# The second attention of a batch runs inside the mixture half of the other batch

## The chip, the cores and the metric

The kernel runs on one core of one Trainium2 chip. The metric is the device time of one execution in microseconds (us), lower is better. The engines are PE (TensorE), DVE (VectorE), ACT (ScalarE), POOL (GpSimd) and SP (SyncE, which here only issues DMAs). Each engine works through its own instructions in order, and waits on semaphores that others raise.

## The reference

Two batches of 1024 tokens, width 256, pass four sublayers, each `x = layernorm(x + f(x))`: a causal attention (16 heads of 128), a mixture of experts, a second attention, and a second mixture.

```python
x = _layernorm(x + _L0_attn_ref(x, ...))
x = _layernorm(x + _L0_ffn_ref(x, ...))      # 8 experts, top 2, plus a shared expert of 704
x = _layernorm(x + _L1_attn_ref(x, ...))
x = _layernorm(x + _L1_ffn_ref(x, ...))      # 16 experts, top 6, plus a shared expert of 352
# second attention: 16 heads of 16, 4 groups of keys and values, no mask
scores = jnp.einsum('bqhd,bkhd->bhqk', q, k) / HD
out = jnp.einsum('bhqk,bkhd->bqhd', jax.nn.softmax(scores, axis=-1), v).reshape(b, s, D)
return out @ Wout + bout
# a mixture: every expert is computed for every token and weighted
h = jax.nn.silu(xf @ W1.T + B1) * (xf @ W3.T + B3)
y = y + c[:, None] * (h @ W2.T + B2)
```

The second attention mixes tokens of one batch only, and a mixture mixes no tokens at all. So work of batch 0 and of batch 1 in different sublayers is independent.

## The kernel before

Every product of near-fp32 precision is made of three fp32r matmuls (`mm3`): each operand is split into a rounded part (`xh`, `hi_gu`, `hh`, rounded by ACT) and the rest (`xl`, `lo_gu`, `hl`, subtracted by DVE or POOL).

The program is a row of stages, each a block that all engines enter and leave together:

- `causal_attention` (a0), both batches.
- `mixture` f0, first batch 0, then batch 1. A tile K is 128 hidden columns of the experts or of the shared expert: 17 tiles for each batch. For each K the weights are loaded, rounded by ACT (`round_gu`, `round_dn`) and subtracted by POOL once, and used for two chunks c of 512 tokens. A chunk of a tile is 18 matmuls of 512 columns: 6 for `gate`, 6 for `up`, 6 for `down`. `gate_ps` and `up_ps` are banks of their own. ACT applies Silu (L1327), DVE multiplies (`product`, L1385) and weighs by the router's map (L1390), ACT rounds (`keep_hi`, L1338), DVE subtracts (`keep_lo`, L1396). Small "side" tasks (norms n0b and n1a, router r0b, projections x0) are done between the chunks, by a plan written out by hand.
- `in_turn` p1: the norm n1b and projections x1 of batch 1, with no other work beside them; SP then copies keys (`x_ks`) and queries (`a_qq`) into their places.
- `grouped_attention` a1: 16 units (batch, 4 heads, 512 queries) of 16 steps. It begins with 24 leading steps of maxima alone (`FIRST`). A step makes the row maxima of a later unit (`maxima`: two matmuls of 512 keys into one of two pairs of banks, one DVE reduction over 1024, L1675), and the transposed scores of this unit (`scores`: two matmuls, L1568, into one of three banks; ACT takes the exponential, L1656). Every second step adds `values` (L1579, four instructions, eight records). In step 9 of a unit (`TURN`) the unit before is normed and the next maxima are transposed.
- `in_turn` p2: output projection o1a, norm n2a and router r1a of batch 0.
- `mixture` f1, batch 0, then batch 1, 25 tiles for each, with the side tasks o1b, n2b, r1b and n3a.
- `in_turn` p3: the last norm and the stores.

What sets the order is each engine's own list; a matmul that waits holds all later ones up.

## Time and profile before

| | us |
|---|---|
| median of 3 runs | 2251.52 (2243.45 to 2257.3) |
| profiled execution, its own time | 2240.75 |
| its span, first to last instruction | 2238.6 |
| PE busy | 2125.4 (95% of the span) |
| DVE busy | 1455.6 (65%) |
| ACT busy | 1207.5 (54%) |
| POOL busy | 556.9 (25%) |

The span is what the trace covers; 2.15 us of the execution lie around it. Busy times of PE overlap from one matmul to the next, so that 95% does not mean that the array is full.

### The profile page before, as it was taken

The numbers are of one execution on the slowest core, as the hardware profiler recorded it, in microseconds if no ns is written. First come the engines' busy times: TensorE is split into PE (matmuls) and PEld (weight loads), VectorE is DVE, ScalarE is ACT, GpSimd is POOL, SyncE is SP. The second block draws the span as 40 slices with busy tenths as digits, with TensorE's granted clock in tenths as the row PEclk, the third lists the DMA queues.
The fourth block names the chain that finished last, engine by engine and source line by source line (L and its number), as shares of the span: only waits on it lengthen the run. The fifth ranks groups of instructions, "written<-read, shape, count | busy, mean of one in ns | idle before, by whom it ended". The sixth has DMA issues, their size and how long they took to land. (4 is left out here: it accounts for less than half of the span.)

```text
span 2238.6 us, 30499 instructions
## 1 busy us (share of the span) xinstructions
PE 2125.4 (95%) x11008; PEld 1608.0 (72%) x11008; DVE 1455.6 (65%) x2505; ACT 1207.5 (54%) x2425; POOL 556.9 (25%) x543
## 2 busy tenths in 40 slices
PE   7999999999999999989999968999998699999998
PEld 5888888888888888867788853333333487787886
DVE  4666666666766666656656547888883656645554
ACT  5655556565656565534444442877777334434344
POOL 3433434343424343322222210000000012221221
PEclk9999999999999999999999995999999799999999
DMA  2000000000000000011111120100000011111111
GB/s 80 15 9 24 15 24 15 24 15 24 8 24 15 24 15 15 6 31 46 43 43 43 43 42 16 23 16 22 16 22 1 27 36 43 43 50 43 48 45 61
DMA packets 54297, 64.74 MB, mean 29 GB/s; under 512 B 9179, under 2 KB 34566, under 8 KB 54150
## 3 DMA queue, kind: packets, MB, share of 16 engines
q1 hardware_dynamic: 54150, 62.81, 10.1%
q8 instruction: 89, 1.46, 0.3%
q14 instruction: 58, 0.48, 0.1%
HBM read 52.68 MB, written 2.10 MB: 24 GB/s over the span
## 5 line engine op out<-in xcount | busy, mean ns | idle before, releaser
L830 POOL TENSOR_TENSOR a_pr<-a_pr,a_rinv 128x128 f32<-128x128 f32 (+7 forms) x256 | 294.2, 1149 | 514.9 <-DVE a_rinv L1063 514.7
L1675 DVE TENSOR_REDUCE a_negm<-psum 128x1 f32<-128x1024 f32 x256 | 301.4, 1219 | 49.2 <-PE psum L1553 48.4
L1227 POOL TENSOR_TENSOR f_lo_gu<-f_raw_gu,f_hi_gu 128x512 fp32r<-128x512 f32 x84 | 108.9, 1296 | 848.4 <-ACT f_hi_gu L1313 848.4
L1656 ACT ACTIVATE a_pt<-psum 128x512 f32<-128x512 f32 x512 | 268.2, 602 | 81.8 <-PE psum L1568 81.5
L86 PE MATMUL psum<-xh,f_hi_gu 128*128 128x512 f32 x672 | 269.4, 401 | 7.0 <-DVE f_hid L1385 6.8
L1396 DVE TENSOR_TENSOR f_hl<-f_hid,f_hh 128x512 fp32r<-128x512 f32 x168 | 116.6, 694 | 236.6 <-ACT f_hh L1338 234.8
L88 PE MATMUL psum<-xh,f_lo_gu 128*128 128x512 f32 x672 | 263.8, 393 | 0.0
L87 PE MATMUL psum<-xl,f_hi_gu 128*128 128x512 f32 x672 | 263.5, 392 | 0.0
L1327 ACT ACTIVATE f_act_s<-psum,f_bias 128x512 f32<-128x512 f32 x168 | 115.1, 685 | 270.6 <-PE psum L88 270.4
L979 ACT ACTIVATE a_pth<-psum 128x512 fp32r<-128x512 f32 (+3 forms) x384 | 174.7, 490 | 142.9 <-PE psum L886 140.5
L972 ACT ACTIVATE a_pr<-psum,a_negm 128x128 f32<-128x128 f32 (+7 forms) x256 | 190.4, 744 | 81.8 <-DVE a_negm L1054 76.9
L1553 PE MATMUL psum<-x_ks,a_qq 48*128 48x512 f32 x512 | 186.3, 475 | 19.3 <-DMA a_qq<-x_qlo 14.5
L1070 DVE TENSOR_TENSOR a_ptl<-psum,a_pth 128x512 fp32r<-128x512 f32 (+3 forms) x384 | 200.3, 549 | 6.1 <-ACT a_pth L979 5.7
L1054 DVE TENSOR_REDUCE a_negm<-psum 128x1 f32<-128x128 f32 (+7 forms) x256 | 189.5, 741 | 2.9 <-PE psum L876 0.7
L1338 ACT ACTIVATE f_hh<-f_hid 128x512 fp32r<-128x512 f32 x168 | 105.5, 628 | 158.9 <-DVE f_hid L1390 151.8
L886 PE MATMUL psum<-ident,a_pr 128*128 128x128 f32 x1152 | 171.8, 276 | 10.7 <-POOL a_pr L830 9.0
L1568 PE MATMUL psum<-a_qq,x_ks 49*128 49x512 f32 x512 | 171.2, 480 | 4.5 <-ACT a_pt L1656 4.1
L1568 PEld LDWEIGHTS psum<-a_qq,x_ks 49*128 49x128 f32 x512 | 67.8, 187 | 138.5 <-ACT a_pt L1656 136.6
L86 PEld LDWEIGHTS psum<-xh,f_hi_gu 128*128 128x128 f32 x672 | 127.3, 189 | 40.2 <-DVE f_hid L1385 10.2
L1385 DVE SCALAR_TENSOR_TENSOR f_hid<-psum,f_bias,f_act_s 128x512 f32<-128x512 f32 x168 | 125.2, 745 | 43.8 <-PE psum L88 33.5
L1091 DVE TENSOR_TENSOR a_zl<-psum,a_zh 128x512 fp32r<-128x512 f32 x64 | 44.2, 691 | 161.5 <-ACT a_zh L1003 161.5
L1553 PEld LDWEIGHTS psum<-x_ks,a_qq 48*128 48x128 f32 x512 | 95.8, 200 | 74.4 <-DVE a_negm L1675 44.5
(299 smaller groups left out, 4823.4 us busy)
## 6 DMA issues: line engine op xcount, KB each, us to landing
f_raw_gu<-in_gu SPq DMA_DIRECT2D x84, 256.0 KB, 2.7
...
a_qq<-x_qhi SPq DMA_DIRECT2D x128, 32.0 KB, 2.0
...
```

Of the source, the lines that this page charges most:

```text
L86: pe.matmul(out, a_hi, b_hi, start=first, stop=False)
L87: pe.matmul(out, a_hi, b_lo, start=False, stop=False)
L88: return pe.matmul(out, a_lo, b_hi, start=False, stop=last)
L830: pool.tensor_tensor(pr[j][:, 0:n], pr[j][:, 0:n], rinv[:, j:j + 1].to_broadcast([P, n]), ALU.mult).then_inc(p_done, 1)
L972: act.activation(pr[qt % NP][:, 0:n], s_ps[:, qt % 2, 0:n], ACT.Exp, bias=negm[:, qt % NP:qt % NP + 1], accum_out=rsum[:, qt % NP:qt % NP ...
L979: act.activation(pth[c][:, rows_of(c, k0, count, qt % CQ), :], t_ps[:, n % 2, 0:count * P].rearrange("p (k q) -> p k q", q=P), ACT.Copy).t ...
L1054: dve.tensor_reduce(negm[:, qt % NP:qt % NP + 1], s_ps[:, qt % 2, 0:n], AX.X, ALU.max, negate=True).then_inc(max_done, 1)
L1070: dve.tensor_tensor(ptl[c][:, p, :], t_ps[:, n % 2, 0:count * P].rearrange("p (k q) -> p k q", q=P), pth[c][:, p, :].bitcast(F32), ALU.sub ...
L1553: m = pe.matmul(mx_ps[:, bank, half, :], qq[p0:p0 + ROWS, u % QSLOT, g % 2, q * P:(q + 1) * P], ks[b][p0:p0 + ROWS, g % 2, half * CH:(half ...
L1568: pe.matmul(st_ps[:, n % 3, :], ks[b][p0:p0 + ROWS + 1, g % 2, kt * P:(kt + 1) * P], qq[p0:p0 + ROWS + 1, u % QSLOT, g % 2, :], start=True ...
L1656: act.activation(pt[:, s % SLOTS, g, :], st_ps[:, n % 3, :], ACT.Exp, scale=1.0 / HD1).then_inc(exp_done, 1)
L1675: dve.tensor_reduce(negm[:, u % 2, g * NQ + q:g * NQ + q + 1], mx_ps[:, bank, :, :], AX.XY, ALU.max, negate=True).then_inc(mx_taken, 1)
```

## The change

In place of the row of stages above, batch 1's half of f0 is merged with batch 0's second attention (a new stage `duet` d0), and batch 0's half of f1 with batch 1's second attention (d1). The other halves stay with `mixture`, now one batch long. The stages are a0, f0 (batch 0), d0, p2, d1, f1 (batch 1), p3. p1 is gone: n1a and x0 are side tasks in the first slots of d0 (`front`), and n1b and x1 are interleaved with o1a, n2a and r1a in p2. o1b, n2b and r1b are side tasks in the last slots of d1 (`rear`, from slot 40).

Inside a duet:

- A slot s is one tile for one chunk of 512 tokens; all tiles are done for chunk 0, then all for chunk 1: 34 slots in d0, 50 in d1. Weights are loaded, rounded and subtracted once for each slot, so twice as often as before. A slot has three parts: `gate(s)`, `up(s)` and `down(s - 1)`, and behind each the side tasks and "beats" of that part.
- A beat is one leading or ordinary step of attention, 24 + 128 in each duet. They are spread evenly over the parts 27 to 101 in d0 (slots 9 to 33, two a part) and 0 to 116 in d1 (slots 0 to 38, 1.3 a part).
- Banks: gate and up share one bank (`gu_ps`), so `up(s)` waits until ACT has read the gate. Maxima have one pair of banks in place of two; each half is reduced by itself (two reductions over 512, joined at the end of a unit by a minimum). Scores have two banks in place of three.
- silu(g) = g/2 (1 + tanh(g/2)): ACT makes g/2 and the tanh (two instructions in place of one), DVE makes `hid` and then `hid1` (two). Weighing (`weigh`) and `keep_lo` move from DVE to POOL.

```diff
+def duet(nc, tag, counters, w, b, xh, xl, yT, ident, idr, psum, router, fore, front, rear, heads, first, last, signals, beat_signals, stale):
...
+    NT = groups * NJ + nsh
+    NCH = S // CH
+    SLOTS = NCH * NT
+    KEEP = 2
+    LAG = 1
-        LAG = 2
-        mx_ps = am.ps([P, 2, 2, CH])
-        st_ps = am.ps([P, 3, CH])
-        acc_ps = am.ps([P, CH])
...
+    LEAD = [(0, i) for i in range(STEPS)] + [(1, i) for i in range(STEPS // 2)]
+    BEATS = [("lead", u, i) for u, i in LEAD] + [("step", u, i) for u in range(END + 1) for i in range(STEPS)]
+    PARTS = 3
+    qhi, qlo, ks, vs, z = heads["qhi"], heads["qlo"], heads["ks"], heads["vs"], heads["z"]
+    qq, pt = heads["qq"], heads["pt"]
+    later = heads["later"]
+    beats = {}
+    for n, beat in enumerate(BEATS):
+        at = first + n * (last - first) // len(BEATS)
+        beats.setdefault((at // PARTS, at % PARTS), []).append(beat)
+    slot_of = {beat: at[0] for at, some in beats.items() for beat in some}
...
+        gu_ps = ph.ps([P, CH])
+        y_ps = ph.ps([P, DT, CH])
+        acc_ps = ph.ps([P, CH])
+        mx_ps = ph.ps([P, 2, CH])
+        st_ps = ph.ps([P, 2, CH])
...
+            def weigh(s):
+                m = SEGMENT[s % NT]
+                if m is not None:
+                    pool.wait_ge(gated, s + 1)
+                    if s >= 1:
+                        pool.wait_ge(hlo_done, s)
+                    pool.tensor_tensor(hid2[:], hid1[:], cmap[:, m, chunk(s)], ALU.mult).then_inc(hid_done, 1)
+            def keep_lo(s):
+                pool.wait_ge(hhi_done, s + 1)
+                pool.tensor_tensor(hl[:, s % 2, :], src_of(s)[:], hh[:, s % 2, :].bitcast(F32),
+                                   ALU.subtract).then_inc(hlo_done, 1)
...
+            for s in range(SLOTS):
+                if s + 1 < SLOTS:
+                    lo_of_gu(s + 1)
+                lo_of_dn(s)
+                weigh(s)
+                keep_lo(s)
...
+            def gate(s):
+                pe.wait_ge(lo_gu_done, s + 1)
+                if s >= 1:
+                    pe.wait_ge(prod_done, s)
...
+            def up(s):
+                pe.wait_ge(tanh_done, 2 * (s + 1))
...
+                n = u * STEPS + i
+                if n >= 1:
+                    pe.wait_ge(mx_taken, 2 * (n - 1) + half + 1)
+                pe.matmul(mx_ps[:, half, :], qq[p0:p0 + ROWS, u % QSLOT, g % 2, q * P:(q + 1) * P],
+                          ks[p0:p0 + ROWS, g % 2, half * CH:(half + 1) * CH], start=True, stop=True).then_inc(mx_ready, 1)
...
-                if n >= 3:
-                    pe.wait_ge(exp_done, n - 2)
-                pe.matmul(st_ps[:, n % 3, :], ks[b][p0:p0 + ROWS + 1, g % 2, kt * P:(kt + 1) * P],
+                if n >= 2:
+                    pe.wait_ge(exp_done, n - 1)
+                pe.matmul(st_ps[:, k, :], ks[p0:p0 + ROWS + 1, g % 2, kt * P:(kt + 1) * P],
                           qq[p0:p0 + ROWS + 1, u % QSLOT, g % 2, :], start=True, stop=True).then_inc(st_ready, 1)
...
+            def step(u, i):
+                ahead_of = maxima_at(u, i)
+                if ahead_of and i == TURN + 1:
+                    if u > 0:
+                        pe.wait_ge(z_done, u)
+                    pe.wait_ge(m_kept, u + 2)
+                for k in range(2):
+                    if ahead_of:
+                        maxima(*ahead_of, k)
+                    if k == 1 and i % 2 == 1 and u * NK + i // 2 >= LAG:
+                        values(u * NK + i // 2 - LAG)
+                    scores(u, i, k)
+                if i == TURN:
...
+            for s in range(SLOTS + 1):
+                for part in range(PARTS):
+                    if s < SLOTS and part == 0:
+                        gate(s)
+                    if s < SLOTS and part == 1:
+                        up(s)
+                    if s >= 1 and part == 2:
+                        down(s - 1)
...
+                    if beats_at(s, part) and not started:
+                        pe.wait_ge(ring.emptied, AHEAD)
+                        started = True
...
+            def tanh(s):
+                act.wait_ge(gate_done, s + 1)
+                if s >= 1:
+                    act.wait_ge(gated, s)
+                k = s % NT
+                act.activation(half_g[:], gu_ps, ACT.Identity, bias=half_b[:, k:k + 1], scale=0.5).then_inc(tanh_done, 1)
+                act.activation(tanh_g[:], gu_ps, ACT.Tanh, bias=half_b[:, k:k + 1], scale=0.5).then_inc(tanh_done, 1)
...
+            def keep_hi(s):
+                if SEGMENT[s % NT] is None:
+                    act.wait_ge(gated, s + 1)
+                else:
+                    act.wait_ge(hid_done, MAPPED[s + 1])
+                act.activation(hh[:, s % 2, :], src_of(s)[:], ACT.Copy).then_inc(hhi_done, 1)
...
+            for s in range(SLOTS + 1):
+                for part in range(PARTS):
+                    if s < SLOTS and part == 0:
+                        tanh(s)
+                    if s + 1 < SLOTS and part == 1:
+                        round_gu(s + 1)
+                    if s < SLOTS and part == 1:
+                        round_dn(s)
+                    if s < SLOTS and part == 2:
+                        keep_hi(s)
...
+                    for beat in beats_at(s, part):
+                        perform(beat)
...
+            def product(s):
+                dve.wait_ge(tanh_done, 2 * (s + 1))
+                dve.wait_ge(up_done, s + 1)
+                dve.scalar_tensor_tensor(out=hid[:], in0=gu_ps, scalar=bias[:, s % NT, 1:2], in1=half_g[:],
+                                         op0=ALU.add, op1=ALU.mult).then_inc(prod_done, 1)
+                dve.wait_ge(prod_done, s + 1)
+                if s >= 1 and SEGMENT[(s - 1) % NT] is None:
+                    dve.wait_ge(hlo_done, s)
+                elif s >= 1:
+                    dve.wait_ge(hid_done, MAPPED[s])
+                dve.scalar_tensor_tensor(out=hid1[:], in0=tanh_g[:], scalar=1.0, in1=hid[:],
+                                         op0=ALU.add, op1=ALU.mult).then_inc(gated, 1)
...
+                for half in range(2):
+                    dve.wait_ge(mx_ready, 2 * n + half + 1)
+                    dve.tensor_reduce(peak[:, u % 2, half, g * NQ + q:g * NQ + q + 1], mx_ps[:, half, :], AX.X, ALU.max,
+                                      negate=True).then_inc(mx_taken, 1)
...
+                dve.tensor_tensor(negm[:, u % 2, :], peak[:, u % 2, 0, :], peak[:, u % 2, 1, :],
+                                  ALU.min).then_inc(m_joined, 1)
...
+            for s in range(SLOTS + 1):
+                for part in range(PARTS):
+                    if s < SLOTS and part == 1:
+                        product(s)
+                    for beat in beats_at(s, part):
+                        perform(beat)
...
-                    mixture(nc, "f0", counters, w0, xh, xl, yT, idr, psum, True, (r0a, r0b), maps(r0a), plan, n1a, (wqkv, x0))
+                    mixture(nc, "f0", counters, w0, 0, xh, xl, yT, idr, psum, r0a, maps(r0a), plan, odd, (), (wqkv, wo, rw1))
...
-                    in_turn(nc, "p1", counters, psum, tasks(n1b, FORE + [("root",)] + BACK) + tasks(x1, PROJECT), (x1, wo, rw1))
-                grouped_attention(nc, "a1", qhi, qlo, ks, vs, z, ident, psum)
+                    n1a = norm(s, "n1a", 0)
+                    x0 = qkv_half(s, "x0", 0, "n1a")
+                    front = norm_slots(n1a) + tasks(x0, PROJECT)
+                    front = {(n // 3, n % 3): [side] for n, side in enumerate(front) if side is not None}
+                    duet(nc, "d0", counters, w0, 1, xh, xl, yT, ident, idr, psum, r0b, maps(r0b), front, {}, heads, 27, 102,
+                         even, beating, (odd,))
...
+                    one = tasks(n1b, FORE) + PAUSE * 2 + [(n1b, ("root",))] + PAUSE * 3 + tasks(n1b, BACK) + tasks(x1, PROJECT)
+                    two = tasks(o1a, TURN + GATHER) + norm_slots(n2a) + PAUSE + tasks(r1a, CHOOSE)
+                    both = [side for pair in zip_longest(one, two) for side in pair if side is not None]
+                    in_turn(nc, "p2", counters, psum, both, (x1,), None, (even, beating))
...
+                    rear = (tasks(o1b, TURN) + PAUSE + tasks(o1b, GATHER) + PAUSE + norm_slots(n2b) + PAUSE +
+                            tasks(r1b, CHOOSE[:2]) + PAUSE + tasks(r1b, CHOOSE[2:]))
+                    rear = {(40 + n // 3, n % 3): [side] for n, side in enumerate(rear) if side is not None}
+                    duet(nc, "d1", counters, w1, 0, xh, xl, yT, ident, idr, psum, r1a, maps(r1a), {}, rear, heads, 0, 117, odd, beating, ())
+                mixture(nc, "f1", counters, w1, 1, xh, xl, yT, idr, psum, r1b, maps(r1b), place(0, norm_slots(n3a, False)), even, (), (),
+                        (n3a, rows, stored, 0))
```

**Place 1, ACT in a slot of d0 without attention** (slot 7). The names f_ are those of a mixture, d_ those of a duet; f_act_s is silu of the gate, d_half_g and d_tanh_g its two parts, f_hh and d_hh the rounded hidden tile. Before, in f1, one tile K of two chunks:

```order
1703 L1327 ACTIVATE f_act_s<-psum,f_bias 128x512 [waits f1_prod_done,f1_gate_done]
1704 L1338 ACTIVATE f_hh<-f_hid 128x512 [waits f1_down_done,f1_hid_done]
1705 L1313 ACTIVATE f_hi_gu<-f_raw_gu 128x512 [waits f1_up_done,f1_raw_gu_in1]
1706 L1338 ACTIVATE f_hh<-f_hid 128x512 [waits f1_down_done,f1_hid_done]
1707 L1327 ACTIVATE f_act_s<-psum,f_bias 128x512 [waits f1_prod_done,f1_gate_done]
1708 L1320 ACTIVATE f_hi_dn<-f_raw_dn 128x256 [waits f1_down_done,f1_raw_dn_in0]
```

After:

```order
1145 L1872 ACTIVATE d_half_g<-psum,d_half_b 128x512 [waits even_gated,even_gate_done]
1146 L1873 ACTIVATE d_tanh_g<-psum,d_half_b 128x512
1147 L1857 ACTIVATE d_hi_gu<-d_raw_gu 128x512 [waits even_up_done,even_raw_gu_in0]
1148 L1864 ACTIVATE d_hi_dn<-d_raw_dn 128x256 [waits even_down_done,even_raw_dn_in1]
1149 L1883 ACTIVATE d_hh<-d_hid 128x512 [waits even_down_done,even_hid_done]
1150 L1872 ACTIVATE d_half_g<-psum,d_half_b 128x512 [waits even_gated,even_gate_done]
```

Before, six instructions serve two chunks, each silu (L1327) reads a bank that only gates are written to, and the hidden tile (L1338) waits for DVE. After, five serve one chunk: the weights are rounded (L1857, L1864) in each slot, and the two instructions on the next gate (L1872, L1873), for which `up` of that slot waits, stand behind `keep_hi` (L1883) of this slot's hidden tile, which waits for `weigh` on POOL (`hid_done`).

**Place 2, PE in a step of attention.** x_ks, x_qq and x_pt are keys, queries and exponentials; L1553/L1748 are maxima, L1568/L1760 scores, L1579/L1770 values. Before, in a1, an odd step with values and the even one behind it:

```order
6522 L1553 MATMUL psum<-x_ks,a_qq 128x512
6523 L1579 MATMUL psum<-a_pt,x_vs 32x512 [waits a1_exp_done]
6524 L1579 MATMUL psum<-a_pt,x_vs 32x512 x3
6525 L1568 MATMUL psum<-a_qq,x_ks 128x512 [waits a1_exp_done]
6526 L1553 MATMUL psum<-x_ks,a_qq 128x512 [waits a1_mx_taken]
6527 L1568 MATMUL psum<-a_qq,x_ks 128x512 [waits a1_exp_done,a1_m_in0]
6528 L1553 MATMUL psum<-x_ks,a_qq 128x512
6529 L1568 MATMUL psum<-a_qq,x_ks 128x512 [waits a1_exp_done]
6530 L1553 MATMUL psum<-x_ks,a_qq 128x512 [waits a1_mx_taken]
6531 L1568 MATMUL psum<-a_qq,x_ks 128x512 [waits a1_exp_done]
```

After, in d1, the end of part 1 of a slot, and part 2 (`down(s - 1)`, and an odd step with a turn), up to the gate of the next slot:

```order
7611 L1748 MATMUL psum<-x_ks,x_qq 128x512 [waits beating_mx_taken]
7612 L1760 MATMUL psum<-x_qq,x_ks 128x512 [waits beating_exp_done]
7613 L87 MATMUL psum<-d_hh,d_hi_dn 128x512 [waits odd_hlo_done,odd_lo_dn_done]
...
7619 L1748 MATMUL psum<-x_ks,x_qq 128x512 [waits beating_mx_taken]
7620 L1760 MATMUL psum<-x_qq,x_ks 128x512 [waits beating_exp_done]
7621 L1748 MATMUL psum<-x_ks,x_qq 128x512 [waits beating_mx_taken]
7622 L1770 MATMUL psum<-x_pt,x_vs 32x512 [waits beating_exp_done]
7624 L1760 MATMUL psum<-x_qq,x_ks 128x512 [waits beating_exp_done]
7625 L1781 MATMUL psum<-ident,d_zt 128x128 [waits beating_z_done,beating_zt_done,beating_mx_taken]
7627 L1790 MATMUL psum<-ident,d_negm 16x128 [waits beating_m_kept,beating_m_joined,beating_mx_taken]
7628 L87 MATMUL psum<-xh,d_hi_gu 128x512 [waits odd_prod_done,odd_lo_gu_done]
```

Before, the second of a step's maxima waits for nothing, and the steps follow on each other. After, each of the two waits for a reduction of its own (`mx_taken`), six matmuls of the mixture stand between the steps, and the next slot's gate stands behind the turn, which waits for the reductions and the joined maxima.

## Rows read from the trace of the kernel before

**Rows 1.** The page: busy time of each engine, share of the span, instructions.

```profile
PE 2125.4 (95%) x11008; PEld 1608.0 (72%) x11008; DVE 1455.6 (65%) x2505; ACT 1207.5 (54%) x2425; POOL 556.9 (25%) x543
```

**Rows 2.** Windows by stage: stretch, length, busy PE, PEld, DVE, ACT, POOL, clock, DMA.

```profile
986.70:995.20 8.50, 4.96 (x16) 2.77 (x16) 3.35 (x5) 1.58 (x3) 1.26 (x1) 0.74 0.57 172
995.20:1157.00 161.80, 159.02 (x702) 126.72 (x702) 101.16 (x182) 70.52 (x124) 39.14 (x38) 0.98 0.15 42
1157.00:1311.00 154.00, 151.74 (x685) 124.38 (x683) 91.98 (x137) 69.88 (x126) 32.25 (x32) 1.00 0.17 43
1311.00:1346.60 35.60, 16.29 (x80) 12.90 (x80) 15.02 (x39) 12.26 (x21) 2.85 (x3) 0.80 0.23 45
1346.60:1377.40 30.80, 25.52 (x49) 11.06 (x47) 27.27 (x24) 1.55 (x2) 0.00 (x0) 0.50 0.11 24
1377.40:1733.00 355.60, 347.59 (x2079) 133.96 (x2079) 284.85 (x265) 278.34 (x543) 0.00 (x0) 0.98 0.07 16
1733.00:1764.70 31.70, 19.30 (x100) 14.58 (x100) 20.98 (x75) 9.80 (x16) 0.00 (x0) 0.85 0.00 1
1764.70:1775.00 10.30, 5.81 (x16) 3.17 (x16) 3.77 (x6) 2.00 (x4) 1.26 (x1) 0.50 0.37 106
1775.00:2016.00 241.00, 238.35 (x1053) 190.15 (x1053) 138.16 (x228) 98.99 (x175) 52.13 (x51) 0.99 0.14 42
2016.00:2226.00 210.00, 209.09 (x922) 170.45 (x920) 113.76 (x167) 87.31 (x160) 48.31 (x48) 1.00 0.16 48
```

**Rows 3.** Timeline of PE in f1: start, duration, instruction.

```profile
2097.87 0.39 PE L86 MATMUL psum<-xh,f_hi_gu 128*128 128x512 f32 x1
...
2100.36 0.39 PE L88 MATMUL psum<-f_hh,f_lo_dn 128*128 128x512 f32 x1
```

**Rows 4.** Timeline of PE in a1, two steps.

```profile
1506.97 0.49 PE L1568 MATMUL psum<-a_qq,x_ks 49*128 49x512 f32 x1
1506.97 0.49 PE L1553 MATMUL psum<-x_ks,a_qq 48*128 48x512 f32 x1
1507.39 1.06 PE L1579 MATMUL psum<-a_pt,x_vs 128*32 128x512 f32 x8
1508.39 0.50 PE L1568 MATMUL psum<-a_qq,x_ks 49*128 49x512 f32 x2
```

**Rows 5.** Timeline of ACT in a1, its last unit: exponentials, without maxima beside them.

```profile
1708.15 2.06 ACT L1656 ACTIVATE a_pt<-psum 128x512 f32<-128x512 f32 x4 [0.55 <-PE psum L1568]
1710.76 2.06 ACT L1656 ACTIVATE a_pt<-psum 128x512 f32<-128x512 f32 x4 [0.54 <-PE psum L1568]
```

**Rows 6.** Groups by form: count, busy us, mean ns, idle before.

```profile
L1675 DVE TENSOR_REDUCE a_negm<-psum 128x1 f32<-128x1024 f32 x256 | 301.4, 1219 | 49.2 <-PE psum L1553 48.4
L1390 DVE TENSOR_TENSOR f_hid<-f_hid,f_cmap 128x512 f32<-128x512 f32 x156 | 142.4, 913 | 5.3
...
L1385 DVE SCALAR_TENSOR_TENSOR f_hid<-psum,f_bias,f_act_s 128x512 f32<-128x512 f32 x168 | 125.2, 745 | 43.8 <-PE psum L88 33.5 <-ACT f_act_s L1327 9.0 <-issue 1.2
...
L1054 DVE TENSOR_REDUCE a_negm<-psum 128x1 f32<-128x512 f32 x32 | 21.5, 671 | 0.0
...
L1327 ACT ACTIVATE f_act_s<-psum,f_bias 128x512 f32<-128x512 f32 x168 | 115.1, 685 | 270.6 <-PE psum L88 270.4
...
L1338 ACT ACTIVATE f_hh<-f_hid 128x512 fp32r<-128x512 f32 x168 | 105.5, 628 | 158.9 <-DVE f_hid L1390 151.8 <-DVE f_hid L1385 7.1
L1313 ACT ACTIVATE f_hi_gu<-f_raw_gu 128x512 fp32r<-128x512 f32 x84 | 52.3, 623 | 13.4 <-DMA f_raw_gu<-in_gu 13.4
...
L1227 POOL TENSOR_TENSOR f_lo_gu<-f_raw_gu,f_hi_gu 128x512 fp32r<-128x512 f32 x84 | 108.9, 1296 | 848.4 <-ACT f_hi_gu L1313 848.4
L1235 POOL TENSOR_TENSOR f_lo_dn<-f_raw_dn,f_hi_dn 128x256 fp32r<-128x256 f32 x84 | 62.7, 746 | 215.5 <-ACT f_hi_dn L1320 215.5
```

**Rows 7.** Tile f_hid: shortest, median and longest weighing, in ns.

```profile
L1390 DVE TENSOR_TENSOR f_hid<-f_hid,f_cmap x156: 691/724/1599, 1001.7 to 2198.2; 128x512 f32<-128x512 f32 x156
```

**Rows 8.** Timeline of PE at the start of a1.

```profile
1345.39 1.23 PE L1553 MATMUL psum<-x_ks,a_qq 48*128 48x512 f32 x4 [14.48 <-DMA a_qq<-x_qlo]
```

More of the change, by code:

```diff
@@ L1214, in _ @@
                     o.sync(sp)
-            for K in range(2, 2 * NT):
+            for K in range(2, NT):
                 load(K)
@@ L1404, in _ @@
             dve.wait_ge(bias_in, 16)
-            for K in range(2 * NT + 1):
+            for K in range(NT + 1):
                 if K >= 1:
@@ new lines, in down, with maxima @@
+            def down(s):
+                if s % NT == 0:
+                    begin_y(s)
+                pe.wait_ge(lo_dn_done, s + 1)
+                pe.wait_ge(hlo_done, s + 1)
+                for dt in range(DT):
+                    d0 = dt * P
+                    i = mm3(pe, y_ps[:, dt, :], hi_dn[:, s % 2, d0:d0 + P], lo_dn[:, s % 2, d0:d0 + P],
+                            hh[:, s % 2, :], hl[:, s % 2, :], False, s % NT == NT - 1)
+                i.then_inc(down_done, 1)
+            def maxima(u, i, half):
```

675 lines of the change are left out of this document (417 added, 258 removed).

## The prediction

> **What bounds the kernel now.** I read the busy times first, then the windows by stage, then the timeline inside the two stages that the change merges, and last the durations by form. PE is busy 95% of the span [rows 1], but the stages differ. In a mixture, matmuls follow each other every 0.227 us (eleven steps in 2.49 us [rows 3]), so a chunk of a tile takes 18 x 0.227 = 4.08 us, and the last half of f1 takes 210 us for 50 chunks, 4.2 each [rows 2]: PE sets it, at full clock, and DVE (54%), ACT (42%) and POOL (23%) have room. In a1 a step takes 1.31 us: the groups of four exponentials of two steps start 2.61 us apart [rows 5]. That is so in the last unit, where DVE has no maxima to reduce, so neither DVE nor PE's own work is the limit. It is a loop: a score is ready for ACT 0.54 us after its issue (0.49 and a handover), the exponential takes 0.60 (four, 0.49 apart, in 2.06 [rows 5]), then come a pair of matmuls (0.43) and the values, 1.0 us from 1507.39 to 1508.39 [rows 4]: 0.54 + 0.60 + 0.05 + 0.43 + 1.0 = 2.62. PE's own work in a step is less, since a score and a maximum run side by side (both start at 1506.97 [rows 4]): 2 x 0.23 + 0.5 = 0.96 us. With turns a step costs 355.6 / 256 = 1.39 us [rows 2].
>
> So there is something to win: 0.35 to 0.43 us of PE in each of 256 steps, about 100 us, and the stages with no dense work (1311 to 1346.6, the 30.8 us of leading maxima, 1733 to 1764.7 [rows 2]). The question is whether a duet can interleave that finely.
>
> **A slot without attention.** Nine slots at the start of d0 and eleven at the end of d1 host none. Before, gate and up had two banks and ACT's silu was off PE's path. Now there is one chain a slot, from the issue of `up(s)`: its result is ready after 5 x 0.227 + 0.39 + 0.05 = 1.58; product 0.75 to 2.33 [rows 6]; `hid1`, by the median weighing 0.72 [rows 7], to 3.1; `weigh` on POOL, by the subtraction of the same shape 1.30 [rows 6], to 4.45; `keep_hi` 0.63 to 5.1; g/2 and tanh, two of 0.685 that overlap a little, to 6.4; then `up(s + 1)`. `down` and the next gate lie inside, and PE idles 2.3 us. The three tiles a chunk of f1's shared expert skip POOL. I add 0.3 for DVE and POOL in each other's way, and 0.3 for side tasks: **7.0 in d0, 6.8 in d1**, against 4.2 before. POOL's product is the one of these without a row of its own: between 0.72, if it took what DVE takes, and 1.60, the longest contended one, the 20 slots move by -12 to +6 us.
>
> `hid1` reads two tensors in SBUF while POOL subtracts weights. The row that is like it is the weighing before: 0.69 at best, 0.91 in the mean, 1.60 at worst [rows 6, 7], so the mean loss is 0.22 us, with POOL busy 23%; in a duet POOL works 1.30 + 0.75 + 1.30 + 1.30 = 4.6 us a slot. The Trainium skill ("SBUF — State Buffer", Who interferes with whom) says that a VectorE instruction with two SBUF inputs blocks fully against a GpSimd one that reads SBUF, whichever comes second. The 1.60 agrees; by that rule the loss would be up to a whole subtraction, and at 0.9 in each of 84 slots the sum would be 50 us higher. I stay with waits of 0.3 to 0.55.
>
> **A joint slot of d1 (3.9 steps).** I lay one out, steps a, b, c, d in parts 0, 1, 2, 2, with b and d having values. Time 0 is the end of `gate(s)` on PE. A reduction over 512 takes 0.67 [rows 6] and starts 0.5 after its matmul.
> - ACT: g/2 and tanh 0.2 to 1.5, then a's exponentials to 2.55. PE: a until 0.5, idle, `up` 1.55 to 2.9. DVE: a's reductions to 1.85.
> - ACT rounds weights (0.62, 0.41) to 3.45. DVE: product to 3.85, then `hid1`, behind POOL's subtraction, 4.45 to 5.2. PE: b with values, to 4.65; `down(s - 1)` to 6.0. b's reductions run 5.2 to 6.45, its exponentials to 5.55.
> - POOL: `lo_dn` to 5.95, `weigh` to 7.25. ACT stands before `keep_hi` until then, and ends it at 7.9. PE: c until 6.75, and d's first score waits for c's exponential, which ACT could only start at 7.9: 8.5. Values, second score: 10.1. Gate: **11.45**. Without the wait for POOL at 4.45 it is 10.8. I take 11.1.
>
> PE's work in it is 4.08 + 3.9 x 0.96 = 7.8; before, the same work took 4.2 + 3.9 x 1.39 = 9.6.
>
> **A joint slot of d0 (six steps, two a part).** Laid out alike, it depends on which step of a part has the values. With the values in the first, they run while DVE reduces: 13.65. With the values in the second, each part ends with 1.0 us of values, a score and then 1.36 us of gate, up or down, in which both maxima banks lie empty and DVE idles 1.5 to 1.8 us: 15.5. The spread of 152 beats over 75 parts gives some 50 steps of the first kind and then the second to the end; the last 24 steps (4 slots) have no maxima, 11.5. PE's work is 9.8, before it was 12.5. DVE (1.5 + 12 x 0.67 = 9.5) and ACT (3.0 + 12 x 0.49 = 8.9) would fit; what costs is that three engines at 60 to 70% wait for each other in order, with one pair of maxima banks and two score banks.
>
> Leading slots: in d0 six leads of 1.3 (a reduction of each half and the refill), product and `hid1`, and three blocks of PE of which DVE idles 0.9 each: 12.5, four of them. In d1 3.9 leads: 8.0, 6.2 slots. A turn's stall was 22.2 - 20.9 = 1.3 us a unit; PE now also waits for the reductions: 1.7, seven in each duet.
>
> **The sum**, against the span of 2238.6:
> - a0 unchanged: 986.7.
> - f0, batch 0: head 8.5 and 161.8 [rows 2], less the maps of r0b (3), plus its last tile's chain, now bare (4): 171.3.
> - d0: head 8.5 and 2 of cold clock; 9 x 7.0 = 63; 4 x 12.5 = 50; 8.3 x 13.65 + 8.4 x 15.5 + 4 x 11.5 = 289; turns 12; the last values, turn and down 8: 432.5. Before: 154 + 35.6 + 30.8 + half of 355.6 = 398, but that held p1 as well.
> - p2: 31.7 before, and n1b and x1 are put between (15 us of DVE [rows 2], and waits of their own): 46.
> - d1: head 10.3, 4 for cold clock and queries; 6.2 x 8.0 = 50; 26.8 x 11.1 + 6 x 10 = 357; turns 12; 11 x 6.8 = 75; end 5: 513. Before: 10.3 + 241 + 177.8 = 429.
> - f1, batch 1: 210 [rows 2], a head of 10.3 and 2 cold: 222.5.
> - p3: 12.6.
>
> That is 2384.6, with the 2.15 around it 2387, and 6.5% over the profiled 2240.75. The median of the runs is 0.5% above that execution, so I forecast **2398 us**. What the change gains (p1 and its 14.5 us wait for queries [rows 8]) is there, and is less than what the slots lose. The least sure terms are the joint slots: 33 and 21 of them, so 1 us a slot is 54 us.
>
> **Rivals.**
> 1. *The interleaving works.* The queues absorb the waits, and a joint slot takes PE's work and 8%: 8.4 and 10.6 to 10.8, leading slots 7.5 and 11, slots without attention 6.5 (that chain is in order on ACT and can't be absorbed), turns 6. d0 is 351, d1 419, the total 2211, by the runs 2221: 1.3% faster. For it: all engines have room, and in a1 a stall is covered by other steps. Against it: each laid out slot has PE waiting for a named bank. It decides at joint slots under 8.6 and 11.0. Chance 0.14.
> 2. *Half of it*: 10 and 12.5 us a slot, 2240 to 2320. Chance 0.23.
> 3. *The forecast*, 2320 to 2460: 0.53.
> 4. *The clock falls in a duet.* While a1 led with maxima alone, PE ran at 0.50, its level of 1.2 GHz, for 30.8 us [rows 2], busy only 25.5 of them by the long records of a slow clock; in the steps behind them it had 0.98. Dense groups of 1.4 to 2.7 us with gaps of 2.3 lie between that and a mixture. At 1.2 GHz a slot without attention costs 2.9 more (up 1.36, and down and gate outlast the chain), leading slots about as much: 30 slots, 90 us, 2490; if joint slots fell too, 2600 and more. The Trainium skill ("TensorE: Matmul & The Clock Gate", What's actually happening) says that the full clock is granted after sustained work and lost after idleness; it leaves open which this is. Chance 0.10.
>
> That the change doesn't do what it says I rule out: the order shows beats in the slots, and no table load between exponentials and tanh.
>
> **How the numbers follow.** About 1% is what a measurement of this kernel tells from no change (the runs spread 0.6%). Faster by over 1% is under 2229: most of rival 1, and a little of 2: 0.14. Within 1% (to 2274): 0.07. Slower: 0.79. The range leaves out rival 1's better part and rival 4: 2240 to 2490.
>
> **What the profile after would show.** Right: d0 430 and d1 510 us long; PE 60 to 75% busy in them; in slots without attention, ACT's `d_hh` waiting for POOL, and about 7 us from `up` to `up`; DVE idle before reductions, released by PE. Wrong: joint slots under 9 us in d1, or PE above 90% there. Wrong the other way: a clock well under 0.9 in the duets.

## The result, and the profile after

The changed kernel takes 2541.78 us (median of four runs, 2535.35 to 2544.78), the kernel before 2250.76 on the same chip: a ratio of 1.129, 95% interval 1.1248 to 1.1332. It is slower, as forecast, but by 291 us and not by 147, and lies above the range. The profiled execution has a span of 2543.0.

The page's busy line (busy us, share of the span, instructions), the answer to [rows 1]: PE's share fell from 95% to 91%, yet its busy time grew by 186 us over as many instructions. Matmuls became longer, not more.

```profile
PE 2311.1 (91%) x11008; PEld 1644.4 (65%) x11008; DVE 1442.7 (57%) x2702; ACT 1306.4 (51%) x2590; POOL 854.0 (34%) x789
```

The windows by stage, with the columns of [rows 2]. The first six lines are d0: head, nine slots without attention, four leading, nine and eight joint ones, the rest. Then come p2 with d1's head, d1 (six leading slots, 33 joint, the tail), and in the last line f1.

```profile
1152.00:1163.20 11.20, 7.73 (x24) 5.42 (x25) 4.13 (x7) 1.58 (x3) 4.05 (x4) 0.60 0.33 95
1163.20:1234.90 71.70, 58.11 (x236) 44.18 (x234) 30.07 (x55) 36.05 (x65) 40.89 (x35) 0.90 0.22 56
1234.90:1310.70 75.80, 60.44 (x127) 31.90 (x127) 37.80 (x59) 12.29 (x24) 19.26 (x17) 0.60 0.16 42
1310.70:1455.20 144.50, 131.96 (x615) 60.94 (x615) 88.48 (x136) 89.21 (x163) 42.58 (x36) 0.97 0.12 34
1455.20:1614.80 159.60, 131.21 (x544) 58.14 (x544) 80.42 (x121) 76.81 (x142) 36.08 (x32) 0.87 0.09 25
1614.80:1685.90 71.10, 61.24 (x237) 28.65 (x237) 7.82 (x14) 38.09 (x70) 16.87 (x15) 0.86 0.03 8
1685.90:1739.40 53.50, 38.46 (x200) 29.23 (x199) 38.05 (x119) 22.19 (x39) 4.12 (x4) 0.86 0.19 40
1739.40:1818.70 79.30, 69.70 (x163) 38.03 (x163) 39.28 (x61) 16.72 (x32) 27.36 (x24) 0.67 0.15 43
1818.70:2212.40 393.70, 358.08 (x1619) 174.94 (x1619) 199.14 (x297) 236.12 (x439) 152.26 (x129) 0.97 0.14 39
2212.40:2296.50 84.10, 66.47 (x292) 50.23 (x292) 37.24 (x67) 37.97 (x70) 43.72 (x39) 0.94 0.13 39
2296.50:2530.40 233.90, 223.32 (x958) 179.68 (x958) 125.32 (x206) 91.84 (x166) 52.13 (x51) 0.96 0.16 47
```

What to see: the joint slots of d0 come in two sorts, 16.1 us each in the fourth line and 20.0 in the fifth, and the clock is 0.97 in one and 0.87 in the other. The leading slots ran at 0.60 and 0.67.

One of the 20 us slots shows both sorts of loss in its middle part. First VectorE, then PE's maxima and values (start, duration, instruction, idle before and its releaser):

```profile
1540.33 0.75 DVE L1957 SCALAR_TENSOR_TENSOR d_hid<-psum,d_bias,d_half_g 128x512 f32<-128x512 f32 x1 [2.35 <-PE psum L89]
1541.11 1.27 DVE L1966 SCALAR_TENSOR_TENSOR d_hid<-d_tanh_g,d_hid 128x512 f32<-128x512 f32 x1
1542.31 2.85 DVE L1977 TENSOR_REDUCE d_peak<-psum 128x1 f32<-128x512 f32 x4
```

```profile
1540.15 0.49 PE L1748 MATMUL psum<-x_ks,x_qq 48*128 48x512 f32 x1
1540.48 0.39 PE L1748 MATMUL psum<-x_ks,x_qq 48*128 48x512 f32 x1
1543.04 0.60 PE L1748 MATMUL psum<-x_ks,x_qq 48*128 48x512 f32 x1 [2.16 <-DVE d_peak L1977]
1543.64 0.79 PE L1748 MATMUL psum<-x_ks,x_qq 48*128 48x512 f32 x1
1544.36 1.94 PE L1770 MATMUL psum<-x_pt,x_vs 128*32 128x512 f32 x8
```

The first beat's maxima fill both banks at 1540.5, but VectorE has the product and `hid1` ahead of their reductions. PE stands 2.16 us before the second beat. Behind the stall it runs at 1.2 GHz: the values take 1.94 us instead of 1.06 [rows 4], and the six matmuls of the `down` that follows 2.85 (1546.95 to 1549.80), where the six of the `up` ahead of the stall took 1.58. VectorE did stand idle during `up` (2.35 us), as forecast; but its next work is then the product, and not a reduction.

Two costs that the prediction had argued over, by tile (shortest, median and longest in ns):

```profile
L1966 DVE SCALAR_TENSOR_TENSOR d_hid<-d_tanh_g,d_hid x84: 691/983/1762, 1167.1 to 2295.1; 128x512 f32<-128x512 f32 x84
L1669 POOL TENSOR_TENSOR d_hid<-d_hid,d_cmap x78: 1259/1272/1303, 1168.2 to 2275.2; 128x512 f32<-128x512 f32 x78
```

### The profile page after: what moved, and what is told of

It is laid out like the page before. It is cut to its first block and busy times, and to the rows that moved or that the text cites. A ratio compares the mean times of both kernels' runs of the same rounds, so it can differ in the third digit from the quotient of the medians.

```text
span 2543.0 us, 31572 instructions
## 1 busy us (share of the span) xinstructions
PE 2311.1 (91%) x11008; PEld 1644.4 (65%) x11008; DVE 1442.7 (57%) x2702; ACT 1306.4 (51%) x2590; POOL 854.0 (34%) x789
## 5 line engine op out<-in xcount | busy, mean ns | idle before, releaser
L1977 DVE TENSOR_REDUCE d_peak<-psum 128x1 f32<-128x512 f32 x512 | 330.2, 685 | 249.6 <-PE psum L1748 249.1
L1917 ACT ACTIVATE x_pt<-psum 128x512 f32<-128x512 f32 x512 | 292.7, 597 | 242.5 <-PE psum L1760 236.7
L1748 PE MATMUL psum<-x_ks,x_qq 48*128 48x512 f32 x512 | 224.4, 500 | 71.6 <-DVE d_peak L1977 61.0
L1760 PE MATMUL psum<-x_qq,x_ks 49*128 49x512 f32 x512 | 231.5, 496 | 16.8 <-ACT x_pt L1917 15.3
L1748 PEld LDWEIGHTS psum<-x_ks,x_qq 48*128 48x128 f32 x512 | 91.4, 204 | 194.0 <-DVE d_peak L1977 125.7
L87 PE MATMUL psum<-xh,d_hi_gu 128*128 128x512 f32 x336 | 160.0, 476 | 40.8 <-ACT d_tanh_g L1873 33.7
L1760 PEld LDWEIGHTS psum<-x_qq,x_ks 49*128 49x128 f32 x512 | 89.5, 192 | 165.5 <-ACT x_pt L1917 108.7
L1770 PE MATMUL psum<-x_pt,x_vs 128*32 128x512 f32 x1024 | 145.3, 641 | 3.5 <-ACT x_pt L1917 1.8
L89 PE MATMUL psum<-xh,d_lo_gu 128*128 128x512 f32 x336 | 143.1, 426 | 0.0
L88 PE MATMUL psum<-xl,d_hi_gu 128*128 128x512 f32 x336 | 143.0, 425 | 0.0
L87 PE MATMUL psum<-a_pth,a_vh 128*128 128x512 f32 (+3 forms) x384 | 134.3, 350 | 6.9 <-DVE a_vl L1111 6.5
L87 PE MATMUL psum<-xh,f_hi_gu 128*128 128x512 f32 x336 | 134.8, 401 | 4.7 <-DVE f_hid L1399 4.7
```

Of the source, the lines that this page charges most:

```text
L87: pe.matmul(out, a_hi, b_hi, start=first, stop=False)
L1748: pe.matmul(mx_ps[:, half, :], qq[p0:p0 + ROWS, u % QSLOT, g % 2, q * P:(q + 1) * P], ks[p0:p0 + ROWS, g % 2, half * CH:(half + 1) * CH], ...
L1760: pe.matmul(st_ps[:, k, :], ks[p0:p0 + ROWS + 1, g % 2, kt * P:(kt + 1) * P], qq[p0:p0 + ROWS + 1, u % QSLOT, g % 2, :], start=True, stop= ...
L1770: m = pe.matmul(acc_ps[g * W:(g + 1) * W, :], vs[:, kt, g, :], pt[:, n % KEEP, g, :], start=kt == 0, stop=kt == NK - 1, tile_position=(0, ...
L1917: act.activation(pt[:, t % KEEP, g, :], st_ps[:, k, :], ACT.Exp, scale=1.0 / HD1).then_inc(exp_done, 1)
L1977: dve.tensor_reduce(peak[:, u % 2, half, g * NQ + q:g * NQ + q + 1], mx_ps[:, half, :], AX.X, ALU.max, negate=True).then_inc(mx_taken, 1)
```

## The experiments

Times are medians of four runs each, ratios are to the kernel before in the same session; "by the ratios" turns a difference of ratios into us with 2250. A slot's length is the distance between the starts of two `half_g`.

**E1, serial.** Is interleaving worth anything against the same duet in series?

```
-        at = first + n * (last - first) // len(BEATS)
+        at = 3 * 9 + 2 if later is not None else 3 * 5 + 2
```

> All 152 attention beats of a duet stand in one place: in d0 behind the last part of slot 9, in d1 behind that of slot 5; every other slot is the mixture's alone. Nothing is left out. If my layout of the slots holds (A: in-order waiting in slots that hold both), d0 is 34 x 7.0 + leads 31 + 128 steps x 1.33 + turns 9 = 450 us and d1 50 x 6.8 + 210 = 550, so d0 is shorter than the measured 533 by 60 to 80 and d1 about the same: total 2455 to 2480. If the clock (B) is what the measured duets lose, the attention alone, which is dense, should show a clock near 0.98 and d0 gain most, with slots without attention at 7.0 to 8.0. If interleaving pays after all, the total rises by over 60 us.

Measured: 2838.42, ratio 1.2648 (1.2599 to 1.2696). Of the three only the last held, a rise of over 60 us, and far beyond its size. Slots without attention are 6.5 us for the most part, but the slot with all the attention in it takes 390.6 in d0 and 389.1 in d1, so some 383 for the beats where I had 210. Windows of it:

```profile
1254.00:1400.00 146.00, 138.01 (x401) 50.63 (x401) 79.61 (x129) 53.71 (x98) 3.74 (x4) 0.51 0.03 7
...
1404.00:1640.00 236.00, 217.67 (x679) 80.68 (x676) 79.86 (x132) 100.78 (x185) 9.40 (x9) 0.53 0.04 10
```

```profile
1340.00:1380.00 40.00, 38.91 (x122) 14.45 (x121) 19.77 (x32) 17.26 (x32) 0.00 (x0) 0.50 0.05 10
```

The clock lay at its level of 1.2 GHz nearly all the time, though the records have PE busy 92 to 97% of it. Before, the same steps ran at 0.98 [rows 2]. So interleaving is worth about 300 us against this series, and the mixture's dense matmuls between the beats go with a clock of 0.97 in the nine joint slots of d0's first sort and in those of d1. The series is not the attention of before, though: its loop has two score banks and one pair of maxima banks, where before there were three and two.

**E2 and E3, the place of the values in a part of d0.**

```
+        at = first + (n + 1) // 2 if later is not None else first + n * (last - first) // len(BEATS)   # E2
+        at = first + n // 2 if later is not None else first + n * (last - first) // len(BEATS)   # E3
```

> d0 alone: exactly two beats in each part, shifted by one, so that the values stand in the first step of a part all through d0 (it ends 2 parts later). By my layout (A) its joint slots take 13.65 by forecast and 16.1 as measured in the first ten of them, against 15.5 and 20: all 21 at 16 makes d0 about 35 to 45 us shorter than 533, the total near 2500. If place within a part does not matter and the 20 us slots come from the clock or from late weights, the total moves by under 12 us.

> The counterpart: exactly two beats in each part of d0, with the values in the second step of a part all through. By (A) the ten slots that took 16.1 us take 20 too: d0 35 to 40 us longer, the total near 2580, and the distance to the kernel with the values first 75 us. If place does not matter, it is within 12 us of the kernel after.

Measured: E2 2499.79, ratio 1.1136 (1.1099 to 1.1173); E3 2581.85, ratio 1.1497 (1.1453 to 1.1542). By the ratios -35 and +47 against the changed kernel, 81 between them. The joint slots with maxima are mostly 15.0 to 16.1 in E2 and mostly 20.3 to 21.0 in E3. The numbers expected, which took the slots' measured sizes, held within 10 us. The same 300 us of d0 in both, E3 first:

```profile
1300.00:1600.00 300.00, 246.45 (x988) 111.14 (x987) 150.59 (x227) 140.77 (x261) 69.24 (x61) 0.86 0.10 27
```

```profile
1300.00:1600.00 300.00, 271.74 (x1247) 127.71 (x1247) 180.08 (x276) 180.43 (x331) 89.04 (x77) 0.96 0.11 31
```

A fourth more matmuls are done in E2. But the clock differs with the place too (0.86, 0.96), so E2 and E3 alone don't say how much of it is waiting and how much clock.

**E4, the queries' fetches spread over slots 7, 8 and 9.**

```
-                    for u in range(QSLOT):
-                        fetch(u)
+                if later is not None and 0 <= s - later["queries"] < QSLOT:
+                    fetch(s - later["queries"])
```

> d0 alone: the 36 query fetches of the first three units are issued 12 in a slot, in slots 7, 8 and 9, with the weight loads between them, instead of all 36 in slot 7. If the queue is what makes slot 9 take 25.1 us (C), that slot falls to some 16 and the one before rises by up to 3: 6 to 10 us off the total. If it is the keys' arrival or the cold clock, slot 9 stays above 20 and the total moves by under 3 us.

Measured: 2539.75, ratio 1.1322 (1.1284 to 1.136): no change. The queue is no longer in the way (ScalarE's wait for this slot's weights is 3.1 us instead of 18.9), but the slot of 25.1 us is still 22.4: its matmuls run mostly at 1.2 GHz. In E2 it is 24.6 and in E8 25.7, both without the spread; in E11, which has all three edits, 14.4. So the queue was one of several things that held this slot, and taking it away alone lets the others show. Which of the other two edits matters beside it was not run.

**E5, multiplications by zero before every `up` and every leading beat.**

```
+            def warm(s, n):
...
+                    for k in range(n):
+                        pe.matmul(y_ps[:, k % 2, :], zero[:], xh[:, k % 2, tokens(s)], start=False, stop=False)
...
             def up(s):
+                warm(s, 6)
...
                     for beat in beats_at(s, part):
+                        if beat[0] == "lead" and (part == 2 and s >= 2 and (s - 1) % NT != NT - 1 or part < 2):
+                            warm(s, 2)
```

> PE multiplies by a matrix of zeros and adds the result to the open y banks, which changes nothing in them: six such matmuls (1.36 us at 2.4 GHz) before each wait of up for the tanh, two before each leading beat of a slot. If the low clock is what the first slots of the duets lose (B), the granted clock of the nine slots at the start of d0 goes from 0.90 to near 1, the leading slots' from 0.60 to above 0.9; slots without attention 7.0, leading ones of d0 13 to 14: d0 25 to 35 us shorter, d1 15 to 20, total 2490 to 2510. If in-order waits alone set the slots (A), the extra matmuls lie in idle time or add to it: total between no change and 40 us longer.

Measured: 2579.57, ratio 1.145 (1.1417 to 1.1482), by the ratios 36 us slower. The clock rose from 0.942 to 0.970 over the span. Nine slots without attention are 72.7 long (71.7 before the edit), four leading ones 76.2 (75.8), in d1 the settled slots 12.2 (10.8): there the 1.36 us of extra work shows in full. The total is as (A) had it, and the clock rose less than (B) asked for (0.94 and 0.84). The window of the 20 us slots, to be held against the changed kernel's fifth line above:

```profile
1455.00:1614.00 159.00, 134.28 (x595) 65.16 (x595) 76.52 (x123) 77.86 (x144) 35.78 (x33) 0.94 0.09 26
```

Same length with more work in it: here the clock must have given back what the zeros took. The same can hold for the leading slots. E9 asks it more cleanly for the 20 us slots.

**E6, the weighing on VectorE.**

```
             def weigh(s):   # no longer called on pool; behind hid1 in the vector block's product:
+                m = SEGMENT[s % NT]
+                if m is not None:
+                    dve.wait_ge(gated, s + 1)
...
+                    dve.tensor_tensor(hid2[:], hid1[:], cmap[:, m, chunk(s)], ALU.mult).then_inc(hid_done, 1)
```

> The weighing of hidden values goes from GpSimd to VectorE, straight behind the product with the tanh. If GpSimd's place in the chain costs what I gave it (D: 1.3 against 0.75 us, a handover, and the wait behind a subtraction), a slot without attention falls from 6.5 by 0.6 and a joint slot of d1 by 0.6 to 1.0: 35 to 60 us off the total. If the reductions (VectorE 70% busy in joint slots) are the limit there instead, the 0.75 us come back as idle PE: within 15 us of the kernel after, with only the 20 slots without attention shorter.

Measured: 2596.55, ratio 1.153 (1.1499 to 1.1562): 54 us slower by the ratios, outside both expectations. Slots without attention fell as expected (5.8 for 6.5), but d0's joint slots of 15 to 16 rose to mostly 17.4 to 19.6, and those of some 20 to as much as 24.1. GpSimd's place in the chain costs 0.7 us in a slot without attention; in the joint slots of d0, 0.69 us more of VectorE ahead of the reductions costs more than it gives back. Part of that is the clock, which fell from 0.97 to 0.89 in the first nine and from 0.87 to 0.81 in the next eight.

**E7, E1 with 60 multiplications by zero ahead of the first step.**

```
+                        if beat == ("step", 0, 0):
+                            warm(s, 60)
```

> The serial kernel (all beats of a duet in one place), with 60 multiplications by zero ahead of the first step of the attention, 26 us at 1.2 GHz and 14 at 2.4. The attention alone ran at 0.50 from its first step to its last, 383 us where the same 128 steps and 24 leads take about 210 at full clock. If the low clock feeds itself (slow matmuls in a chain of waits are not dense enough to lift it), a lifted clock stays up over most of the steps: 150 us less in each duet, total near 2550. If the chain's gaps bring it down at any speed (two score banks and one pair of maxima banks instead of three and two), it falls back within some 10 us and the total is 2838 plus up to 40.

Measured: 2856.07, ratio 1.2675 (1.2639 to 1.2711), no better than E1. The clock did rise, and fell back after 20 us, in windows and in PE's timeline:

```profile
1293.00:1303.00 10.00, 8.59 (x43) 3.10 (x41) 7.82 (x13) 6.59 (x12) 0.00 (x0) 1.00 0.00 0
1303.00:1313.00 10.00, 8.29 (x38) 3.25 (x37) 7.14 (x12) 6.44 (x13) 0.00 (x0) 0.97 0.00 1
1313.00:1318.00 5.00, 5.00 (x17) 1.89 (x16) 2.19 (x5) 1.78 (x4) 0.00 (x0) 0.50 0.02 4
```

```profile
1297.60 1.06 PE L1777 MATMUL psum<-x_pt,x_vs 128*32 128x512 f32 x8
...
1308.20 1.06 PE L1777 MATMUL psum<-x_pt,x_vs 128*32 128x512 f32 x8
...
1310.53 0.50 PE L1755 MATMUL psum<-x_ks,x_qq 48*128 48x512 f32 x1 [0.62 <-ACT d_mrow L1904]
...
1311.81 0.50 PE L1755 MATMUL psum<-x_ks,x_qq 48*128 48x512 f32 x1 [0.55 <-DVE d_peak L1987]
...
1313.13 1.93 PE L1777 MATMUL psum<-x_pt,x_vs 128*32 128x512 f32 x8
...
1318.32 1.93 PE L1777 MATMUL psum<-x_pt,x_vs 128*32 128x512 f32 x8
```

At full clock three pairs of steps take 10.60 us (from the values at 1297.60 to those at 1308.20), 1.77 us a step, where before it was 1.31 [rows 5] and, with turns, 1.39: this loop is slower at any clock. Right behind two waits of 0.6 us at the turn the clock is down, and from then a pair of steps takes 5.19. Once down it stays there (0.51 from 1313 to 1640); lifting it once is no cure.

**E8, product and `hid1` between the reductions of the middle part's two beats.**

```
-                    if s < SLOTS and part == 1:
+                    some = beats_at(s, part)
+                    behind = len(some) > 1 and not side_at(s, part)
+                    if s < SLOTS and part == 1 and not behind:
                         product(s)
...
+                    for n, beat in enumerate(some):
+                        if s < SLOTS and part == 1 and behind and n == 1:
+                            product(s)
```

> VectorE's product and hid1 stand between the reductions of the two beats of the middle part, not ahead of both. In the 20 us slots PE waited 2.16 us for VectorE before the second beat's maxima, and VectorE had stood idle from the end of up. If such in-order waits are what a joint slot is made of (A), the slots of d0 fall by 1.0 to 2.0, those of d1 that have two beats in the middle part by 0.5 to 1.0: 30 to 60 us off the total. If the wait is only moved (the next part's maxima wait instead, or GpSimd's weighing comes too late for keep_hi), within 12 us.

Measured: 2481.01, ratio 1.1028 (1.0995 to 1.1062): 59 us faster than the changed kernel by the ratios, the largest gain of one edit, and its instructions are the same. The 20.4 us slots of d0 are 16.0, 4.4 less where 1.0 to 2.0 were expected; three leading ones are 13.7 to 14.8 instead of 16.5 to 17.8, three slots of d1 11.2 or 11.3 instead of 14.3 to 15.9. The clock rose too, to 0.98 in the window of 1458 to 1600, where it had been 0.86. VectorE in such a slot:

```profile
1494.67 0.68 DVE L1977 TENSOR_REDUCE d_peak<-psum 128x1 f32<-128x512 f32 x1
1495.27 0.74 DVE L1957 SCALAR_TENSOR_TENSOR d_hid<-psum,d_bias,d_half_g 128x512 f32<-128x512 f32 x1
1496.05 0.69 DVE L1966 SCALAR_TENSOR_TENSOR d_hid<-d_tanh_g,d_hid 128x512 f32<-128x512 f32 x1
1496.66 1.28 DVE L1977 TENSOR_REDUCE d_peak<-psum 128x1 f32<-128x512 f32 x2
```

**E9, zeros only where PE stands idle: five, in the middle part of d0's slots, ahead of the second beat.**

```
+                        if n == 1 and part == 1 and later is not None and (s - 1) % NT != 0:
+                            warm(s, 5)
```

> Five multiplications by zero (1.1 us at 2.4 GHz) stand only where PE stands idle in d0: in the middle part, between the first beat and the maxima of the second. Earlier, six of them before every up lifted the clock of the 20 us slots from 0.87 to 0.94 and left their length as it was. If the clock (B) has a price of its own there, which was only eaten up by the 1.36 us of extra work, these slots now fall by 1.0 to 2.0 us each, d0 by 15 to 35. If they don't move, the low clock fills time that PE would wait anyway.

Measured: 2520.76, ratio 1.1208 (1.1166 to 1.1251), by the ratios 18 us less; the two intervals touch, but the slots of the trace say it plainly: 20.4 became 17.6. The same 142 us, the changed kernel first, then E9:

```profile
1458.00:1600.00 142.00, 117.19 (x485) 51.97 (x477) 70.80 (x107) 67.60 (x126) 31.58 (x28) 0.86 0.09 26
```

```profile
1458.00:1600.00 142.00, 125.12 (x580) 58.22 (x578) 78.02 (x119) 75.52 (x141) 36.26 (x32) 0.99 0.11 29
```

The order and the waits of the other work are as they were, so 2.8 us of a 20.4 us slot is the price of the low clock alone, more than the 1.0 to 2.0 expected. By this, of the 4.4 us that E8 takes off the slot some 2.8 are clock and 1.6 the wait itself. The Trainium skill ("TensorE: Matmul & The Clock Gate", A second HAM failure mode: psum-queue depth-cycling) tells of short idle times between groups of matmuls, from cycling through PSUM banks, that make the clock swing between its two levels. These slots agree: the clock is 0.86 in the mean, and in the stretch shown above it goes from 1.00 to 0.50 within 1543 to 1544 and is back by 1551. In E1 the lower level was held, with no swing to speak of, through nearly the whole of 383 us.

**E10, reductions over half of each bank** (it leaves out half of the keys in the maxima).

```
-... mx_ps[:, half, :], AX.X, ALU.max,
+... mx_ps[:, half, 0:CH // 2], AX.X, ALU.max,
```

> Each reduction reads 256 of the 512 scores of its half, so the maxima are taken over half of the keys (this leaves out part of the computation): some 0.42 us instead of 0.686, 512 of them, 136 us of VectorE work less. By (A), where PE and VectorE wait for each other in turn with one pair of maxima banks, a slot of d0 with twelve reductions falls by 2 to 3.2 us, one of d1 by 1 to 2, leading slots by 2 to 3: total 90 to 130 us shorter. If ACT's order or the clock holds the slots, under 40.

Measured: 2500.46, ratio 1.1111 (1.1077 to 1.1146), 40 us less by the ratios and less than half of what (A) had asked for. The 20.4 us slots are 18.1 to 20.0, the 16 us ones 14.7 to 15.6, d1's settled ones 10.8 as before. The edit takes 133 us of work off VectorE (a reduction takes 0.419 us instead of 0.685) and the total falls by 40. So VectorE's amount of work counts, but for less than the order in which it does it: E8, with no work less, is worth 59.

**E11, E2 + E4 + E8 together.**

> Three edits together: values first all through d0, product and hid1 between the two beats, the queries' fetches spread over three slots. The first alone took 42 us off, the third 2. If the waits add up slot by slot, the second brings what it brings alone: 2540 - 42 - 2 - (30 to 60) = 2435 to 2465. With the values in the first step the product's place may be worth nothing, since VectorE then reduces beside the values: 2490.

Measured: 2454.58, ratio 1.0917 (1.0876 to 1.0957): 84 us less than the changed kernel by the ratios, within the expectation. Joint slots with maxima are mostly 14.5 or 15.5. A stretch of nearly six of them, and one part of one:

```profile
1468.40:1555.80 87.40, 82.14 (x398) 38.72 (x391) 54.20 (x89) 57.10 (x105) 25.96 (x24) 1.00 0.11 30
```

```profile
1486.24 0.50 PE L87 MATMUL psum<-xh,d_hi_gu 128*128 128x512 f32 x1
...
1487.83 0.50 PE L1748 MATMUL psum<-x_ks,x_qq 48*128 48x512 f32 x1
1487.83 0.49 PE L1760 MATMUL psum<-x_qq,x_ks 49*128 49x512 f32 x1
1488.16 0.39 PE L1748 MATMUL psum<-x_ks,x_qq 48*128 48x512 f32 x1
1488.49 1.06 PE L1770 MATMUL psum<-x_pt,x_vs 128*32 128x512 f32 x8
1489.48 0.75 PE L1760 MATMUL psum<-x_qq,x_ks 49*128 49x512 f32 x2
1489.82 0.64 PE L1748 MATMUL psum<-x_ks,x_qq 48*128 48x512 f32 x2
1490.66 0.50 PE L1760 MATMUL psum<-x_qq,x_ks 49*128 49x512 f32 x1 [0.21 <-ACT x_pt L1917]
1491.09 0.50 PE L87 MATMUL psum<-xh,d_hi_gu 128*128 128x512 f32 x1
```

PE is busy 94% at full clock. From 1486.24 to 1487.83 it does `up`, then in 3.26 us two steps with one short wait: 1.63 a step. Three parts of 4.85 are the 14.5 us slot.

**E12, E11 with `keep_hi` between the exponentials of the last part's two beats.** The edit is E8's pattern, in ScalarE's loop and part 2.

> The combined kernel, with ScalarE's keep_hi between the exponentials of the two beats of the last part, not ahead of both. ScalarE waited 156 us for GpSimd's weighing there. If these waits hold back the exponentials and with them PE, as in-order waiting (A) has it, a joint slot falls by 0.3 to 1.0 us: 2455 less 15 to 50. If PE's own row of matmuls sets the slots of 14.5 by now (four 3.4 us pairs of steps hold 93% of PE), the total stays within 10 us, or rises, since hh is then later for keep_lo and down.

Measured: 2452.43, ratio 1.0939 (1.0904 to 1.0974), the same as E11. ScalarE's wait for GpSimd went from 156.0 to 116.9 us, and its wait for scores rose from 151.1 to 189.6. This fits slots that PE's own row of matmuls sets by now; no run shortened that row, so it is argued and not shown. No version of the duet beat the kernel before.

## Why the prediction was wrong

The profiled span is 158.4 us above the sum of 2384.6. By its terms:

- *f0, p2 and heads, f1.* f0 165.3 for 171.3; p2 with d1's head 53.5 for 60.3; f1 with its head 229.5 (from 2300.9) for 222.5. Together -6: right.
- *A slot without attention, 7.0 and 6.8*: right as a mechanism. Undisturbed ones take 6.5 (E1). In d0 nine took 71.7 for 63, with the clock at 0.90; d1's tail 88.5 for 80. `weigh` on POOL takes 1.27 (estimate 1.30). `hid1` has a median of 0.98, longest 1.76, where I had 0.72 plus waits of 0.3 to 0.55: about that. +17 in all.
- *Joint slots of d1, 11.1 and 10*: 32.8 of them with the turns took 393.7 for 369.5, +24. A part with one beat came out as laid out (slots of 10.8); those with two in the middle part had the wait that E8 takes away.
- *Leading slots, 12.5 and 8.0*: 75.8 for 50 in d0 and 79.3 for 50 in d1, +55. I had put VectorE's product among the idle times of three blocks of PE, at full clock. They ran at 0.60 and 0.67, and my own rows had the leads of before at 0.50 [rows 2]. Half of d0's excess is its first leading slot, 25.1 us, where 36 fetches of queries, issued over 24 us, stood ahead of the weights; the sum had nothing for that (E4, E11). In the other three E8 gives back about 3 us each. What the clock alone costs here isn't settled: E5 raised it to 0.84 in d0 at the same length, and from 0.75 to 0.93 in d1's first nine slots for 6 us (112 for 118), but the zeros added some 4 us of work to a leading slot of d0 and 2 to one of d1, which can have hidden a gain. What is left of this term was not taken apart.
- *Joint slots of d0, 13.65 and 15.5*: **this is the step that failed**, 375.2 for 309 with turns and end, +66. I had the kinds right, and that they differ by the place of the values (E2 and E3). Their sizes were 16.1 and 20.0. I wrote that with the values second "both maxima banks lie empty and DVE idles"; the trace shows banks that are full while VectorE does the product first, and PE waiting 2.16 us behind them. E8 brings the second kind to 16.0. Of the 4.4 us between, 2.8 are the clock (E9), which the layout had at full speed.

Behind this stands a number that I took too small: "PE's own work in a step is less", 0.96 us. I had argued from the last unit of a1, which has no maxima, that this work isn't the limit. In the kernel before, four steps with maxima take 5.20 us at full clock, from the values at 1504.80 to those at 1510.00, and the records have PE busy all the time (the ends of matmuls are modelled, so that this is a sign and no proof):

```profile
1504.80:1510.00 5.20, 5.20 (x33) 2.02 (x33) 4.64 (x5) 3.82 (x9) 0.00 (x0) 1.00 0.02 6
```

So the 1.31 us of before were near PE's own row already, and "0.35 to 0.43 us of PE" to win in a step were not there. In the duet a step takes more: 1.63 us in the best order that I ran (E11), where a maximum runs alone ahead of the values and the second score waits 0.21 us for its bank, and 1.77 in the serial loop at full clock (E7). By 1.63 a joint slot of d0 is 4.1 + 6 x 1.63 = 13.9, by 1.31 it would be 12.0; rival 1 (10.6 to 10.8) asked for 1.1 us a step, less than any run here took. Whether the 0.3 us between are the price of one pair of maxima banks and two score banks is open: no run gave a bank back.

Rival 4, the clock, came in part: in the leading slots of both duets, and in d0's second kind of joint slot, where I had no price for it outside a "2600 and more". I treated it as a case apart. It is a multiplier on the waits: each wait removed (E8) also took away slow matmuls. The sign that I had named for this, a clock well under 0.9, stood in the leading slots; d0 took 534 us and not 430.

The direction was right for the reason given: waits in order that cost more than the removed stages gave. That the order makes them is shown (E2, E3, E8); what the fewer banks add is not.
